# Squares of two slabs side by side on TensorE, and the request for the fields moved ahead

## What is computed

```python
def _cin_layer(x0, x, kernel):
    W = kernel.reshape(m, h_prev, kernel.shape[1])
    return jnp.einsum('bmd,bhd,mho->bod', x0, x, W)
x = x0
for k in (k1, k2, k3):
    x = _cin_layer(x0, x, k)
    finals.append(jnp.sum(x, axis=-1))
logit = jnp.concatenate(finals, axis=-1) @ kf
```

## Time and profile before

| | us |
|---|---|
| median of 3 runs | 327.26 |
| lowest, highest | 326.59, 328.71 |
| profiled execution | 325.52 |
| its span from first to last instruction | 323.6 |
| mean granted clock of TensorE in it | 0.984 of full speed |

### The profile page before, as it was taken

How to read it: one execution, slowest core, us unless ns; L and a number is a source line. 1 busy time by engine, 2 the same in 40 slices (tenths; PEclk the granted TensorE clock), 3 DMA queues, 4 the chain that set the end, 5 groups by cost and what they waited for, 6 DMA issues and landing times.

```text
span 323.6 us, 7268 instructions
## 1 busy us (share of the span) xinstructions
PE 312.4 (97%) x2888; PEld 86.6 (27%) x2888; DVE 197.8 (61%) x220; ACT 147.6 (46%) x131; POOL 153.8 (48%) x70
## 2 busy tenths in 40 slices
PE   8977699999999999999999999999999999999996
PEld 3322122222222222222222222222222222222221
DVE  4632747775665667776665666776665666776631
ACT  1304534555454444555454444555444444555511
POOL 1230654555544444555544444555544444555500
PEclk9997599999999999999999999999999999999999
DMA  7947999999999977788777777888777777610010
GB/s 239 403 147 229 367 372 403 385 338 350 358 364 327 321 286 286 309 319 303 292 287 272 258 268 285 311 316 306 287 289 278 253 271 284 267 32 19 17 32 1
DMA packets 18231, 86.82 MB, mean 268 GB/s; under 512 B 3756, under 2 KB 4012, under 8 KB 9260
## 3 DMA queue, kind: packets, MB, share of 16 engines
q1 hardware_dynamic: 15640, 77.68, 63.8%
q10 hardware_dynamic: 2548, 8.99, 10.0%
q0 software_dynamic: 32, 0.00, 0.0%
HBM read 86.12 MB, written 0.53 MB: 268 GB/s over the span
## 4 chain that ended last, share of the span: by engine, by line
PE 91%; DMA 5%; DVE 2%; SPq 1%; issue 0%; ACT 0%; ACTq 0%; DVEq 0%
PE acc L489 67%; PE rot L473 10%; PE acc L495 10%; PE acc L520 3%; DMA t_tab<-ts 2%; DMA v<-v_rows 2%; DVE prod L410 1%; DMA tr<-t_tab 1%; PE acc L528 0%; SPq L208 0%; SPq L209 0%; DVE xy L416 0%; ACT ysb L258 0%; DVE sums L418 0%; DVE ts L422 0%
## 5 line engine op out<-in xcount | busy, mean ns | idle before, releaser
L489 PE MATMUL acc<-prod,w 128*32 128x512 f32 x2048 | 229.5, 599 | 1.2 <-DVE prod L410 1.1
L326 POOL TENSOR_TENSOR prod<-u,v 128x1024 f32<-128x1024 f32 x64 | 151.6, 2392 | 144.7 <-PE acc L495 125.4
L489 PEld LDWEIGHTS acc<-prod,w 128*32 128x32 f32 x2048 | 63.3, 110 | 159.5 <-issue 151.5
L416 DVE TENSOR_TENSOR xy<-acc,ysb 128x512 f32<-128x512 f32 x32 | 22.1, 691 | 99.8 <-ACT ysb L258 99.8
L243 ACT ACTIVATE prod<-rot 128x1024 f32<-128x1024 f32 x64 | 65.7, 1027 | 36.0 <-DVE prod L410 22.9
L410 DVE TENSOR_TENSOR prod<-rot,u 128x1024 f32<-128x1024 f32 x64 | 77.7, 1214 | 6.1 <-DMA v<-v_rows 5.7
L410 DVE TENSOR_TENSOR prod<-rot,v 128x1024 f32<-128x1024 f32 x64 | 77.6, 1212 | 0.0
L258 ACT ACTIVATE ysb<-acc,kf 128x512 f32<-128x512 f32 x32 | 22.0, 687 | 114.4 <-PE acc L495 114.4
L247 ACT ACTIVATE feat<-u 128x2048 f32<-128x2048 f32 x32 | 60.9, 1902 | 12.2 <-issue 8.2
L473 PE MATMUL rot<-xc,picks 32*128 32x512 f32 x256 | 37.4, 655 | 1.5 <-DVE prod L410 1.5
L495 PE MATMUL acc<-feat,wf 64*32 64x512 f32 x512 | 35.7, 614 | 2.2 <-issue 2.2
(11 more groups left out here) (28 smaller groups left out, 12.5 us busy)
## 6 DMA issues: line engine op xcount, KB each, us to landing
u<-u_rows SPq DMA_DIRECT2D x31, 1024.0 KB, 4.9
v<-v_rows SPq DMA_DIRECT2D x31, 1024.0 KB, 6.9
xc<-x_chunks SPq DMA_DIRECT2D x32, 256.0 KB, 5.0
feat<-u_rows ACTq DMA_DIRECT2D x32, 256.0 KB, 3.2
u<-u_rows SPq DMA_DIRECT2D x2, 512.0 KB, 7.6
v<-v_rows SPq DMA_DIRECT2D x2, 512.0 KB, 9.2
prod<-k3f SPq DMA_DIRECT2D x1, 544.0 KB, 4.0
prod<-k3f SPq DMA_DIRECT2D x1, 512.0 KB, 5.4
```

The costliest lines, as they stand in the source:

```text
L326: nc.gpsimd.tensor_tensor(prod[p][:, UV, pair(half)], us[n][:, pair(half)], vs[n][:, pair(half)], ALU.mult).then_inc(uv_ready, 2)
L416: nc.vector.tensor_tensor(xy[p][:], acc[p][0][:], ysb[p][:], ALU.mult).then_inc(xy_ready, 1)
L489: nc.tensor.matmul(acc[p][h][quad(c), :], w[:, t, h * G:(h + 1) * G], prod[p][:, t, chunk(c)], start=(t == first), stop=False, skip_group_ ...
```

## The change

On PE, an even slab's contraction no longer opens or closes its accumulators with its first tile or squares: its squares have been issued at the end of the odd step before, right behind the odd slab's own, with start set (features(1 - p, opens=True)). The even slab's last contraction matmul closes the accumulators and signals acc_ready. For that, an odd step waits before its last tile also for xy_ready of the slab before (the accumulators must be free), for feat_ready of the next slab and for feat_in of the next slab. Step 31 has no next slab, and slab 0 stays as it was. On ACT, place_fields moves ahead of the wait for products and the second square_w.

```diff
@@ ACT, step
                     square_fields(s + 1, q, m)
+                    place_fields(s + 1, q)
                     act.wait_ge(products_ready, 4 * (s + 1) + 2)
                     square_w(s + 1, q, 1)
-                    place_fields(s + 1, q)
@@ PE
-            def contract(s, h, p, tiles, first, count=None):
+            def contract(s, h, p, tiles, first):
...
-                    if h == 1 and t == VW and count is not None:
-                        pe.wait_ge(feat_ready, s + 1)
-                        pe.wait_ge(feat_in[p], count)
                     for c in range(CHUNKS):
-                        nc.tensor.matmul(acc[p][h][quad(c), :], w[:, t, h * G:(h + 1) * G], prod[p][:, t, chunk(c)],
-                                         start=(t == first), stop=False, skip_group_check=True)
-
-            def features(p):
+                        mm = nc.tensor.matmul(acc[p][h][quad(c), :], w[:, t, h * G:(h + 1) * G], prod[p][:, t, chunk(c)],
+                                              start=(t == first), stop=(first is None and t == tiles[-1]),
+                                              skip_group_check=True)
+                return mm
+
+            def features(p, opens=False):
                 for h, rows in ((0, slice(2 * M, 4 * M)), (1, slice(0, 2 * M))):
                     for c in range(CHUNKS):
-                        mm = nc.tensor.matmul(acc[p][h][quad(c), :], wf[rows, :], feat[p][rows, chunk(c)], start=False,
-                                              stop=True, skip_group_check=True)
-                mm.then_inc(acc_ready, 1)
+                        mm = nc.tensor.matmul(acc[p][h][quad(c), :], wf[rows, :], feat[p][rows, chunk(c)], start=opens,
+                                              stop=not opens, skip_group_check=True)
+                if not opens:
+                    mm.then_inc(acc_ready, 1)
@@ PE, step
+                tiles = (UV, WW, UW, VW)
                 wait(pe, xy_ready, s - 1)
-                for h in range(2):
-                    contract(s, h, p, (UV, WW, UW, VW), UV, 32 * it + 16 * (n // 2 + 1))
+                if n % 2 == 0:
+                    contract(s, 0, p, tiles, None)
+                    contract(s, 1, p, tiles, None).then_inc(acc_ready, 1)
+                    return
+                contract(s, 0, p, tiles, UV)
+                contract(s, 1, p, tiles[:-1], UV)
+                pe.wait_ge(feat_ready, s + 1)
+                pe.wait_ge(feat_in[p], 32 * it + 16 * (n // 2 + 1))
+                more = not isinstance(s, int) or s + 1 < SLABS
+                if more:
+                    pe.wait_ge(xy_ready, s)
+                    pe.wait_ge(feat_ready, s + 2)
+                    pe.wait_ge(feat_in[1 - p], 32 * it + 16 * ((n + 1) // 2 + 1))
+                contract(s, 1, p, tiles[-1:], UV)
                 features(p)
+                if more:
+                    features(1 - p, opens=True)
```

## The result

| | before | changed |
|---|---|---|
| median of the runs, us | 326.92 | 343.46 |
| lowest, highest | 323.39, 328.71 | 342.26, 344.05 |
| ratio, 95% interval | | 1.0539 [1.0474, 1.0604] |
| span of the profiled execution | 323.6 | 341.8 |

The change makes the kernel 5.4% slower (the ratio is that of the means of the fast runs, which leaves out the 328.71 us of before). The forecast was 346 us (5.8% over the median it started from).

A forecast was written before the change was run, and what follows sets the result against it. PE, busy 97% of the span, was taken to bound the kernel. Stalls of 9.8, 10.5 and 1.0 us less a gain of 2.4 made + 18.9 on 325.5, 344.4; with the median's 1.7, 346 us, range 337 to 356.

The forecast's parts named there:

- deadline of C + 6.04: In odd steps, PE needs the next slab's fields 6.04 us after the contraction's start, for the last tile's matmuls.
- request at C + 3.06: ACT asks for the fields 3.06 us after the odd step's contraction starts, about 0.1 us after its squares.
- stall = L - 2.9: PE's wait per odd step: time from the fields' request to their landing, minus 2.9 us.
- The gain: Squares of two slabs issued together on PE save 0.16 us a pair, over 15 pairs 2.4 us.
- upper bound of 3.8: Saving of 0.25 us a pair, 3.8 us, if going from contraction straight into rotation is cheaper too.
- Steps 1, 3, 5: Early odd steps, PE waiting for fields behind SP's full load queue: stalls 3.0, 4.1 and 2.7, together 9.8 us.
- the 20 us ahead: Sign in the profile after: the DMA share of 1.0 ends some 20 us earlier than before the change.
- rival 2: Clock falls to half in the early stalls; + 5 to + 10 over the forecast, about 352, at most 356 us; chance 0.14.
- Steps 7 to 25: Ten later odd steps: fields land 3.95 us after their request, so PE stalls 1.05 us each, 10.5 us.
- The straight line between (1.2, 3.1) and (3.9, 4.4): Points pair xc's landing after the fields' request with the fields' landing time; read at 2.95 us, it gave 3.95 us.
- Rival 1: In late odd steps the fields still land 3.1 us after request; steps 7 to 29 cost 2.4 to 3; 338 us; chance 0.20.
- Rival 4: ACT's small request is served in turn with SP's long queue, landing in 3.1 us from the start; 328.5 us; chance 0.04.

The follow-up runs named there:

- Half the loads: The changed kernel with v not loaded from slab 4 on, u fetched in two halves, products using an old v: 329.87 us, ratio 1.0096.
- the later wait: The changed kernel with the three next-slab waits moved between the two sets of squares and PE's loop written out: 330.11 us, ratio 1.0097.
- the written-out loop: The changed kernel with PE's loop written out step by step and nothing else: 350.25 us, ratio 1.0672.

## Why the prediction was right

**The place of the loss.** As forecast, PE waits in the contraction of odd steps for the transfer of the fields, nowhere else. The deadline of C + 6.04 and the request at C + 3.06 were right to 0.1 us: in step 7 the request is at 109.82 - 106.71 = C + 3.11. stall = L - 2.9 holds: 3.97 gives 1.07, the stage lost 1.12.

**The gain.** 2.4 us forecast, 15 x 0.15 to 0.17 = 2.3 to 2.6 found (squares side by side 1.88 us). Contraction straight into rotation is not cheaper than into squares, so the upper bound of 3.8 was too generous.

**Steps 1, 3, 5.** Forecast 3.0 + 4.1 + 2.7 = 9.8; found 3.0 + 4.8 + 0.9 = 8.7, and 2.9 of half clock. Step 3's L was 7.6 where I had drawn the 7.4 of the same transfer down to 7.0. Step 5's is the mis-sized one: the queue had nothing left over, because steps 1 and 3 together lost 10.7 us and not 7.1, and the queue drained all that time. L was 3.8, not 5.6. The DMA share of 1.0 ended at 78 us, earlier than the 20 us ahead that I had forecast (in the kernel before it was still 0.99 from 93 to 102 us). So rival 2 came true in one of three places, and it paid part of itself back in step 5, as its paragraph said.

**Steps 7 to 25.** The term sized worst: 1.05 each, 10.5 in sum; found 0.4 to 1.1, some 7 us. The loads did land where I had put them (xc 2.2 to 3.0 us after the request; I said 2.95), but L there is 3.3 to 4.0, 3.55 in the mean, not 3.95. The straight line between (1.2, 3.1) and (3.9, 4.4) had a bad far end. That point is a single transfer, the one of 116.20 us in the kernel before. Its queue (q10) in the DMA view from 116.1 to 118.4 us and from 118.4 to 121 us (packets, MB, share):

```profile
q10 hardware_dynamic: 40, 0.25, 40.3%
```

```profile
q10 hardware_dynamic: 8, 0.02, 2.6%
```

30 of its 32 packets of 8 KB started within 2.0 us of the request, as in the settled steps behind it; only the last two were late, by 1.0 and 1.7 us. So the 4.4 does not tell what four microseconds of loads do to the whole transfer. Step 7 of the changed kernel, L 4.0, has such a late pair too. Rival 1 (no effect at all) was half right. Errors of opposite sign leave the sum at 18.2 against 18.9: 3.8 us too much over steps 7 to 29 and 1.1 over steps 1 to 5, against 2.9 of clock and 1.5 of start-up that were not in it. That the total is this close is luck.

**Rival 4 and the page behind it.** The Trainium skill (DMA: Bandwidth & Descriptors, Queues, rings and completion order) says that each DMA engine goes round its queues packet by packet. The trace disagrees with the rule taken as a promise for a small request: in step 3 of the changed kernel, requested at 65.05 us, ACT's queue (q10) moves its first packet at 68.5. From 65.4 to 68.0 us it has none, while SP's (q1) moves a megabyte:

```profile
q1 hardware_dynamic: 162, 1.04, 99.5%
```

Whether the packets of the request were in their queue by then, the trace does not tell. Half the loads gave 3.0 instead of 7.6 us in the same step.

**The margin.** The chances (0.92 for slower) rested on L never being under 2.9 us. In 22 transfers from 100 us on, of the changed kernel, it was 2.9 to 4.0, and in the odd steps, which are those that wait, 3.1 or more:

```profile
DMA to landing us min/median/max: 2.9/3.1/4.0
```

## What to carry to other kernels

Before you let the bounding engine wait for something one stage earlier, subtract: the earliest landing of it from the new deadline, once in a settled stretch and once where the load queue is full. A saving of 0.16 us a pair can't pay for a wait of 0.3; make the input local (here a 1.9 us copy on an engine with room), and the same saving makes the kernel 1% faster. Putting the wait after the last work that doesn't need it took back most of the loss (330.1 us), but not all: the wait of 2.9 us in step 3, with the half clock behind it, alone cost 4.8 us, and the kernel stayed 1% slower than before. And a stall isn't charged once: it drains queues (less to wait for later) and can drop the clock (more).

## What the runs showed of the hardware

- The landing of 256 KB on ACT's queue takes 2.8 to 3.4 us where the last of the other loads lands at most 1.2 us after the request or there are hardly any (the kernel before from 125 us on, half the loads from 56 us on), 3.3 to 4.0 where it lands 2.2 to 3.0 us after it (changed kernel, steps 7 to 25), and 6.4 to 7.9 under a DMA share of 1.0 (the kernel before from 40 to 107 us; step 3 of the changed kernel 7.6, with the later wait 7.9).
- Two of the 32 packets of such a transfer can start 0.5 to 2.5 us behind the others, and the landing comes late with them (the step of 112 us before, step 7 of the changed kernel, step 9 of the written-out loop).
- In the stall of 4.6 us the granted clock fell to 0.50 and stayed there to 79 us; behind one of 2.8 us (written-out loop, step 9) it fell too. In the 3.05 us of step 1 it did not (1.00 from 50 to 60 us), nor in 1.9 us in step 13 of the written-out loop, nor in any stall under 1 us. The length of the gap alone does not tell.
- A loop of PE written out cost 4 to 7 us in a kernel whose PE waits for transfers, with 14 more packets of instructions.
- A stage with a stall under 1 us is longer by some 0.2 us beyond what PE's idle time shows (1.12 against 0.91 in step 7, 0.84 against 0.63 in step 9).
